# Cross attention with a routed FFN on one Trainium2 core: keys stacked by 12 transfers of four heads, q stacked through DRAM by 4, raw weights loaded later in the turn

## The reference

```python
x = x + xattn(layernorm(x), ctx)            # q and out: rows and weights quantized to 8-bit integers
    # q = w8a8(x, wq, bq); k = ctx @ wk.T + bk; v = ctx @ wv.T + bv     (16 heads of 32)
    # attn = softmax(q @ k.T / sqrt(32) + mask); out = w8a8(attn @ v, wo, bo)
x = x + moe(layernorm(x))
    # probs = softmax(h @ router_w.T); two best experts per token, their weights made to sum to 1
    # out += weight * (silu(h @ gate.T) * (h @ up.T)) @ down.T
```

## Time and profile before

| | |
|---|---|
| median of 3 runs | 1627.09 us (1625.84 to 1628.61) |
| the profiled execution | 1627.48 us, span of its instructions 1625.8 us |
| PE busy | 1506.3 us, 93% |
| DVE, ACT, POOL busy | 58%, 54%, 45% |
| attention loop (score matmuls) | 61.7 to 1118.4 us |
| experts | from 1168.7 us |
| moved by DMA | 281.53 MB, mean 173 GB/s |
| mean granted TensorE clock | 0.974 |

### The profile page before, as it was taken

One profiled execution on the slowest core, in us unless ns is written; L12 is line 12 of the kernel. 1 busy time (PEld: TensorE's weight loads), 2 busy tenths in 40 slices (PEclk: granted clock), 3 DMA queues, 4 the chain that ended last, 5 costly groups with the idle time before them and its releaser, 6 DMA issues. The chain is left out here.

```text
span 1625.8 us, 40635 instructions
## 1 busy us (share of the span) xinstructions
PE 1506.3 (93%) x11593; PEld 1312.3 (81%) x11594; DVE 944.7 (58%) x2675; ACT 878.9 (54%) x2128; POOL 731.8 (45%) x798
## 2 busy tenths in 40 slices
PE   2899999999999999999999999995299999999796
PEld 2788888888888888888888888874299999999695
DVE  6567777777777777777777777765222222222121
ACT  2466666666666666666666666664033333333232
POOL 4234444543445434543444434542445555555352
PEclk9999999999999999999999999997599999999898
DMA  6667777677667777677766776668147766575543
GB/s 201 171 171 204 202 207 184 176 220 199 188 178 193 208 201 185 175 219 197 192 180 188 213 201 187 175 178 264 33 77 181 184 162 142 141 171 121 134 78 46
DMA packets 219151, 281.53 MB, mean 173 GB/s; under 512 B 82080, under 2 KB 163872, under 8 KB 219104
## 3 DMA queue, kind: packets, MB, share of 16 engines
q1 hardware_dynamic: 200928, 247.78, 54.2%
q0 software_dynamic: 18176, 33.17, 11.4%
HBM read 118.12 MB, written 66.77 MB: 114 GB/s over the span
## 5 line engine op out<-in xcount | busy, mean ns | idle before, releaser
L500 ACT ACTIVATE probs<-probs,neg_max 112x375 f32<-112x375 f32 x512 | 311.8, 609 | 235.2 <-DVE neg_max L576 229.1
L576 DVE CUSTOM_DVE_ANT_0 probs<-score,neg_mask 112x375 f32<-112x375 f32 x512 | 279.3, 545 | 195.9 <-PE score L729 179.7
L493 ACT ACTIVATE probs_t<-turn 125x336 f32<-125x336 f32 x512 | 225.0, 440 | 99.8 <-PE turn L737 99.4
L737 PE MATMUL turn<-ident,probs 112*125 112x112 f32 x1536 | 265.7, 282 | 2.7 <-ACT probs L500 2.7
L737 PEld LDWEIGHTS turn<-ident,probs 112*125 112x125 f32 x1536 | 223.6, 189 | 37.6 <-issue 19.1
L729 PE MATMUL score<-k_stack,q_stack 96*112 96x376 f32 x512 | 208.5, 407 | 4.3 <-DMA q_stack<-q_lo 3.4
L764 PE MATMUL proj<-down_hi,gate_up_hi 128*128 128x376 f32 x512 | 176.2, 344 | 14.9 <-DVE gate_up_lo L601 13.7
L978 POOL DMA_INDIRECT out<-y_rows,entries x63 | 102.2, 1622 | 175.0 <-ACT y_rows L1004 136.9
L1016 DVE TENSOR_TENSOR a_lo<-a_ps,a_hi 128x384 fp32r<-128x384 f32 x63 | 35.1, 558 | 250.9 <-ACT a_hi L991 159.0
L764 PE MATMUL proj<-down_hi,gate_up_lo 128*128 128x376 f32 x512 | 172.1, 336 | 0.0
L764 PE MATMUL proj<-down_lo,gate_up_hi 128*128 128x376 f32 x512 | 172.0, 336 | 0.0
(11 more groups left out here) (195 smaller groups left out, 3552.7 us busy)
## 6 DMA issues: line engine op xcount, KB each, us to landing
k_stack<-gate_up_hi SPq DMA_DIRECT2D x512, 94.0 KB, 2.1
k_stack<-gate_up_lo SPq DMA_DIRECT2D x256, 94.0 KB, 2.1
ctx_stage<-ctx_t SPq DMA_DIRECT2D x32, 750.0 KB
q_stack<-q_hi SPq DMA_DIRECT2D x256, 56.0 KB, 2.0
w_raw<-gate_up_t SPq DMA_DIRECT2D x32, 352.0 KB, 3.1
gate_up_dram_hi<-w_hi SPq DMA_DIRECT2D x32, 352.0 KB
gate_up_dram_lo<-w_lo SPq DMA_DIRECT2D x32, 352.0 KB
gate_up_hi<-gate_up_dram_hi SPq DMA_DIRECT2D x16, 704.0 KB, 6.6
```

What stands on the lines that cost most here:

```text
L493: act.activation(probs_t[:, h % RING_T, :, :], turn[h % 2][0:LC, 0:LT * N].rearrange("p (l n) -> p l n", l=LT), ACT.Copy).then_inc(turned_ ...
L500: act.activation(probs[:, h % DS, :], probs[:, h % DS, :], ACT.Exp, bias=neg_max[:, par % 2, h:h + 1], scale=-1.0, accum_out=total[:, par ...
L576: dve.tensor_tensor_reduce(probs[:, h % DS, :], score[h % 2][0:N, 0:L], neg_mask[:, p, :], 1.0, BIG, ALU.add, ALU.min, neg_max[:, p, h:h + ...
L737: mm = pe.transpose(turn[h % 2][0:LC, l * N:(l + 1) * N], probs[:, h % DS, l * LC:(l + 1) * LC], W["ident"][0:N, 0:N])
```

## The change

Keys are stacked four heads at a time, by `stack_keys(i)` with three transfers for the heads 4i to 4i + 3. These four heads lie in the same 32 partitions, one in each key unit: the host orders the rows of wk, wq and their biases so that partition group i of all four units holds heads 4i to 4i + 3. Group 3 of element a is stacked at the top of turn a, groups 0, 1 and 2 of n in the middle, each when the four scores that read its place are done; all of them need all four key units. k_stacked becomes four semaphores of 3 transfers each, and ACT waits for all four before it writes k_hi at g = 0. q_hi and q_lo lie in one tile, which one transfer copies to DRAM between k(0) and k(1); three transfers of 32 partitions bring it back into q_st when the copy has landed. ACT waits for the copy (q_kept) before it writes q_hi again. The two loads of w_raw move from before neg_mask to behind x_res.

```diff
--- before.py
+++ after.py
@@ -210,7 +210,7 @@
                 mm.then_inc(row_made, 1)
 
 
-def attention(nc, W, R, x, ctx_t, mask, x1, h2, slots):
+def attention(nc, W, R, x, ctx_t, mask, x1, h2, slots, q_dram):
 
 
 
@@ -228,7 +228,7 @@
     UNITS = KT + LT
     GH = 4
     DS, RING_T = 4, 2 * GH
-    KDMAS, QDMAS = 12, 12
+    KDMAS, QDMAS = 3, 3
 
     with ExitStack() as ctx:
         sb = lambda name, shape, dt=F32: ctx.enter_context(nc.sbuf_tensor(name, shape, dt))
@@ -241,7 +241,8 @@
         stage, c_hi, c_lo, x_in = W["stage"], W["c_hi"], W["c_lo"], W["x_in"]
         k_hi, k_lo = [W[f"k_{part}"][:, 0:G4 * LP].rearrange("p (g l) -> p g l", g=G4) for part in ("hi", "lo")]
         k_st = sb("k_stack", [96, H, LP], F32R)
-        q_hi, q_lo = sb("q_hi", [128, G4, N], F32R), sb("q_lo", [128, G4, N], F32R)
+        q_parts = sb("q_parts", [128, 2, G4, N], F32R)
+        q_hi, q_lo = q_parts[:, 0, :, :], q_parts[:, 1, :, :]
         q_st = sb("q_stack", [96, 2, H, N], F32R)
         v = sb("v", [LC, 2, LT, C])
         neg_mask = sb("neg_mask", [N, 2, L])
@@ -290,10 +291,11 @@
 
         c_hi_made, c_lo_made = W["c_hi_made"], W["c_lo_made"]
         unit_made, unit_out = sem("unit_made"), sem("unit_out")
-        k_hi_made, k_stacked = sem("k_hi_made"), [sem("k_stacked0"), sem("k_stacked1")]
+        k_hi_made, k_stacked = sem("k_hi_made"), [sem(f"k_stacked{i}") for i in range(4)]
         ln1, rstd_made = sem("ln1"), sem("rstd_made")
         q_made, q_out = sem("q_made"), sem("q_out")
         q_biased, q_hi_made, q_stacked = sem("q_biased"), sem("q_hi_made"), sem("q_stacked")
+        q_kept = sem("q_kept")
         mask_negated = sem("mask_negated")
         scored, masked, softmaxed = sem("scored"), sem("masked"), sem("softmaxed")
         turned, turned_out, valued = sem("turned"), sem("turned_out"), sem("valued")
@@ -343,13 +345,12 @@
 
         @block.sync
         def _(sp):
-            def stack_keys(half):
-
-                for i in range(4):
-                    rows = slice(QUARTER * i, QUARTER * i + QUARTER)
-                    for r, src in ((0, k_hi), (1, k_lo), (2, k_hi)):
-                        sp.dma_start(k_st[QUARTER * r:QUARTER * r + QUARTER, 8 * half + i:8 * half + 8:4, :].bitcast(F32),
-                                     src[rows, 2 * half:2 * half + 2, :].bitcast(F32)).then_inc(k_stacked[half], 16)
+            def stack_keys(i):
+
+                rows = slice(QUARTER * i, QUARTER * i + QUARTER)
+                for r, src in ((0, k_hi), (1, k_lo), (2, k_hi)):
+                    sp.dma_start(k_st[QUARTER * r:QUARTER * r + QUARTER, G4 * i:G4 * i + G4, :].bitcast(F32),
+                                 src[rows, :, :].bitcast(F32)).then_inc(k_stacked[i], 16)
 
             def body(it, par, inside=False):
                 has_m2, has_m, has_a, has_n, has_nn, has_n3 = stages(it, inside)
@@ -359,11 +360,8 @@
                     if inside or it > 0:
                         waited(sp)
                         need(sp, scored, H * it)
-                    stack_keys(1)
+                    stack_keys(3)
                 if has_n:
-                    need(sp, w_lo_made, n)
-                    sp.dma_start(w_raw[:, 0:WG], W["gate_up_flat"][:, bass.ds(n * WG, WG)]).then_inc(w_in, 16)
-                    sp.dma_start(w_raw[:, WG:WG + WD], W["down_flat"][:, bass.ds(n * WD, WD)]).then_inc(w_in, 16)
                     need(sp, masked, H * (n - 1))
                     sp.dma_start(neg_mask[:, (par + 1) % 2, :], mask[n, :, :]).then_inc(mask_in, 16)
                 if has_m2:
@@ -375,18 +373,24 @@
                     need(sp, x1_steps, 2 * m)
                     sp.dma_start(x_res[:, :], x[m, :, :]).then_inc(x_res_ld, 16)
                 if has_n:
+                    need(sp, w_lo_made, n)
+                    sp.dma_start(w_raw[:, 0:WG], W["gate_up_flat"][:, bass.ds(n * WG, WG)]).then_inc(w_in, 16)
+                    sp.dma_start(w_raw[:, WG:WG + WD], W["down_flat"][:, bass.ds(n * WD, WD)]).then_inc(w_in, 16)
+                if has_n:
                     q = (par + 1) % 2
-                    need(sp, unit_out, UNITS * n + KT // 2)
-                    if has_a:
-                        waited(sp)
-                        need(sp, scored, H * it + H // 2)
-                    stack_keys(0)
-                    need(sp, q_out, 3 * n + 3)
-                    for i in range(4):
-                        rows = slice(QUARTER * i, QUARTER * i + QUARTER)
-                        for r, src in ((0, q_hi), (1, q_hi), (2, q_lo)):
-                            sp.dma_start(q_st[QUARTER * r:QUARTER * r + QUARTER, q, i:H:4, :].bitcast(F32),
-                                         src[rows, :, :].bitcast(F32)).then_inc(q_stacked, 16)
+                    need(sp, unit_out, UNITS * n + KT)
+                    for i in range(3):
+                        if has_a:
+                            waited(sp)
+                            need(sp, scored, H * it + G4 * (i + 1))
+                        stack_keys(i)
+                        if i == 0:
+                            need(sp, q_out, 3 * n + 3)
+                            sp.dma_start(q_dram[n, :, :, :], q_parts[:, :, :, :].bitcast(F32).rearrange("p a g n -> p a (g n)")).then_inc(q_kept, 16)
+                    need(sp, q_kept, 16 * (n + 1))
+                    for r, part in ((0, 0), (1, 0), (2, 1)):
+                        sp.dma_start(q_st[QUARTER * r:QUARTER * r + QUARTER, q, :, :].bitcast(F32).rearrange("p (i g) n -> p i (g n)", g=G4),
+                                     q_dram[n, :, part, :].rearrange("(i p) f -> p i f", p=QUARTER)).then_inc(q_stacked, 16)
                 if has_n3 and (inside or n3 > 0):
                     need(sp, c_lo_made, n3)
                     need(sp, c_hi_made, n3)
@@ -403,8 +407,8 @@
                     sp.wait_ge(unit_out, UNITS * B)
                     sp.wait_ge(w_stored, 64 * B)
                     load_expert(sp, R, 0)
-                    for half in range(2):
-                        sp.wait_ge(k_stacked[half], 16 * KDMAS * B)
+                    for i in range(4):
+                        sp.wait_ge(k_stacked[i], 16 * KDMAS * B)
                     load_expert(sp, R, 1)
 
             iterations(sp, body)
@@ -511,8 +515,9 @@
                     if h in (3, 5, 7, 9) and has_n:
                         g = h // 2 - 1
                         need(act, unit_made, UNITS * n + g + 1)
-                        if g % 2 == 0:
-                            need(act, k_stacked[g // 2], 16 * KDMAS * n)
+                        if g == 0:
+                            for i in range(4):
+                                need(act, k_stacked[i], 16 * KDMAS * n)
                         act.activation(k_hi[:, g, :], proj[(par + 1 + g) % 2][:, 0:LP], ACT.Identity,
                                        bias=W["bk_col"][:, g:g + 1]).then_inc(k_hi_made, 1)
                     if has_a:
@@ -528,7 +533,7 @@
                                        ACT.Copy).then_inc(r_out, 1)
                     if h == 9 and has_n:
                         need(act, q_made, 3 * n + 3)
-                        need(act, q_stacked, 16 * QDMAS * n)
+                        need(act, q_kept, 16 * n)
                         act.activation(q_hi[:, :, :], misc[:, 0:G4 * N].rearrange("p (g n) -> p g n", g=G4),
                                        ACT.Identity).then_inc(q_hi_made, 1)
                     if h == 10 and has_nn and (inside or nn > 0):
@@ -721,8 +726,8 @@
         def _(pe):
             def scores(b, par, h):
                 k = b * H + h
-                if h % 8 == 0:
-                    need(pe, k_stacked[h // 8], 16 * KDMAS * (b + 1))
+                if h % G4 == 0:
+                    need(pe, k_stacked[h // G4], 16 * KDMAS * (b + 1))
                 if h == 0:
                     need(pe, q_stacked, 16 * QDMAS * (b + 1))
                 need(pe, masked, k - 1)
@@ -1139,7 +1144,7 @@
                                                                         "slots_cleared", "pads_cleared")})
             prepare_weights(nc, W, x, ctx_t, wq, wk_t, wv_t, wo, bq, bk, bv, bo, router_t, slots, h2, out[T:T + PAD_ROWS, :])
             attention(nc, W, R, x, ctx_t, mask, out[0:T, :].rearrange("(b n) c -> b n c", n=N),
-                      h2[0:T, :].rearrange("(b n) c -> b n c", n=N), slots)
+                      h2[0:T, :].rearrange("(b n) c -> b n c", n=N), slots, dram("q_parts_dram", (B, 128, 2, C // 128 * N)))
         experts(nc, W, R, h2, slots, out)
 
 
@@ -1155,9 +1160,10 @@
 
     turn = lambda a, *axes: np.ascontiguousarray(np.transpose(np.asarray(a), axes))
     whole = lambda a: np.ascontiguousarray(np.asarray(a))
+    by_chunk = lambda a: np.asarray(a).reshape(4, 4, -1).swapaxes(0, 1).reshape(np.asarray(a).shape)
     arrays = {
         "x": whole(x), "ctx_t": turn(ctx_2048, 0, 2, 1), "mask": whole(mask_BxSxS2_ff0),
```

(2 more changed lines are left out.)

## The result

The changed kernel takes 1799.63 us (median of 4 runs, 1793.39 to 1801.81) against 1626.46 us for the kernel before, run beside it: a ratio of 1.106, 95% interval 1.103 to 1.109. The prediction was 1691 us with a range of 1642 to 1748. Slower was right, for the reason given; the size was not, and the result is outside the range. The profiled execution took 1799.6 us with a span of 1797.9, the one before 1627.5 and 1625.8, so 172.1 us are to be explained.

A forecast was written before the change was run, and what follows sets the result against it. PE's work was taken to bound the attention loop. The profiled 1627.5 us, plus 64.8 for the gaps (30 x 2.0 + 4.8) as k(3) lands late, less 1.6 at the end, gave 1691 us; range 1642 to 1748.

The forecast's parts named there:

- (e): ACT's k_hi write at h = 3 now waits for all four stackings; DVE's low part and PE wait behind it.
- (f): SP's queue, moved in order, lands k(3) 21.7 us after the fourth result; low part 2.0 us late each turn.
- 0.2 late, inside the 2.0: q loads land 0.2 us after the score matmul's time, within the 2.0 us stall per turn and not on top.
- The first gap and the end: First gap between fourth and next first result grows 4.8 us; expert loads reached earlier at the end give -1.6 us.
- The clock, a rival at 0.32: PE's clock falls behind its pauses in the loop, losing 1.7 us in each of 31 turns, 53 us: 1744; chance 0.32.
- (a): SP's issuing: 24 key and 12 q transfers become 12 and 4; worth nothing inside the loop.
- the first rival: No stall: above 272 GB/s into 32 partitions k(3) is in time and the change no slower, 1627; chance 0.12.
- (b): Two raw weight loads issued behind the mask, the x1_s and h2_s stores and the x_res load: nothing.
- (c): Host order of the weights' rows, q_lo and q_hi in one tile: same instructions and shapes, nothing.
- (d): ACT waits before q_hi for the copy to DRAM, which comes before the old stacking: nothing.
- faster: Third rival: line 601 at h = 3 comes earlier, PE's 0.4 us per turn goes, 12 us in all: 1614; chance 0.06.

The follow-up runs named there:

- with q ahead: Changed kernel with its three q loads issued ahead of k(2), k(3) left at the top of the next turn: 1864.59 us, 1.142 of before.
- the kernel with the order mended: Changed kernel with k(3) issued at the end of the turn before and the q loads ahead of k(2): 1623.66 us, 0.998 of before.
- the swap on DVE: Kernel before with DVE's two operations at h = 3 exchanged, the keys' low part ahead of h2_s: 1610.78 us, 0.990 of before.

## Why the prediction was right or wrong

**(e), the wait that moves: right.** ACT waits at h = 3 for k_stack in 25 turns (57.1 us), DVE and PE behind it (57.2 us, some 70 predicted), and the chain hangs on the fourth result of the turn before. The wait alone on the kernel before (1863.5) and k(3) a turn earlier (1708) show it from both sides.

**(f), when k(3) lands: the failed step.** 21.7 us were predicted from the fourth result to k(3)'s landing, and a gap of 22.9. Measured are 23.7 us to the last byte, some 24.3 to the landing (ACT's write begins at 928.44, 24.3 after 904.12), and a gap of 25.5. Two terms were too small.

First the way to k(3)'s first byte: 18.6 us in the sum (21.7 less 2.5 for k(3)'s data and 0.6 for its landing), 19.5 in the trace. By the times of the single pieces (medians over 27 turns) this is lost at the head of the chain: k(0)'s 0.58 MB last from 1.4 to 4.9 us behind the fourth result, 3.6 us where 2.5 were taken, and the copy ends at 6.4 instead of 5.1. Why k(0) is slow stays open. From there on the stretches are as long as they were taken: k(1) and k(2) end at 11.1 (10.0 in the sum), q's loads at 14.1 (13.0). So the 230 GB/s, from 154 GB/s divided by a share of 0.64 and its like, were too much for k(0) (205) and not for k(1) and k(2) (238). The Trainium skill, SBUF — State Buffer, section on the DMA port swizzle, has 218 GB/s as the asymptote into 32 partitions; k(0) stays under it, k(1) and k(2), six such transfers one behind the other into three groups of 32 partitions, do not. For such a train the measured 238 decides.

Second and larger, k(3) itself: 2.5 us at 230 GB/s, measured 4.2 (its first piece begins 19.5 us behind the fourth result, its last ends at 23.7). "SP's transfers are moved in order" is what failed. In the stretch from 923.6 to 927.8 the engines move 257 GB/s x 4.2 us = 1.08 MB, of which k(3) has 0.58. The mask and the store of x1_s, issued behind it at 921.72 and 923.45, move 0.35 MB beside it, which at 257 GB/s is 1.4 of the 1.7 us; the other 0.15 MB are the last of the weight stores ahead of it. With the raw weights behind it as well k(3) ends 0.9 us later. The Trainium skill, DMA: Bandwidth & Descriptors, section on queues, rings and completion order, says that on each DMA engine descriptors are consumed in ring order but a later one may finish its write first, and that completion is not in order for an issuing engine; the trace agrees as far as it goes (mask pieces move from 925.5 on, k(3)'s last one begins at 927.2), and shows that this has a price for the earlier transfer.

**"0.2 late, inside the 2.0": half right.** q was 2.1 us late in the turn (score matmul 15.3 us behind the fourth result, not 13.2): its loads ended 14.1 us behind it instead of 13.0, and from the last byte to the matmul it is 1.2 us, of which the prediction had 0.4. But inside the chain it was: with q ahead the gaps stay, and only the place of the pause changes.

**The first gap and the end.** +4.8 was predicted for the first gap, 7.1 measured; -1.6 for the end, -4.6 measured behind the last score matmul. The last element was forgotten, with its wait for q and its clock (+4.9). Together they make little.

**The clock, a rival at 0.32: real, but of another size.** It was priced at 1.7 us in each of 31 turns, 53 us, and cost 24 us in 7 turns through the stretches, as most falls of the clock began before k(3)'s pause. The 108.9 us between the sum (1690.7) and the profiled execution (1799.6) are 82.8 us of gaps (147.6 less 64.8), 24.2 of the stretches that the clock made longer, and 1.9 behind the last result (0.3 instead of -1.6).

**(a) "worth nothing": wrong for the chain.** On the kernel before only q's part of it was run alone (0.997); the keys' part was not. Where the chain starts at the fourth result, transfers of 94 KiB cost 69 us more. So coalescing, which the Trainium skill, DMA: Bandwidth & Descriptors, rules for kernel authors, advises, did help here; but the first rival ("above 272 GB/s") fell with the 205 and 238 measured. **(b) "Nothing": the same.** Moving the raw loads gives 0.999 alone on the kernel before; with the new wait in place it is worth 65 us. Both terms were priced by the slack of the kernel before, which step (e) of the same prediction had used up. **(c), (d): right**, as the kernel with the order mended, at 0.998, holds them all.

**The sign.** For faster there was 0.07. Its mechanism exists, though the change doesn't use it: the swap on DVE shows that PE's 0.4 us per turn are to be had (1.0%).

## What to carry to other kernels

When a change makes a wait stand on the last transfer of a chain, price every other part of the change again in that chain: transfers issued just behind it slow it, and the time to issue those ahead counts. A rate seen with idle engines, divided by their share, is no measurement: 240 GB/s was worked out so, and 205 and 238 came. And before removing one of two pauses, ask where the clock's fall behind the remaining one will lie: order the queue by who waits first (here q, k(2), k(3), then loads and stores), which removes both.

## What had not been expected of the hardware

Pauses of PE of about 2 us in an otherwise full loop already bring its clock to half (behind 1.8 to 2.0 us in about every second turn, with k(3) a turn earlier), and a longer one costs more. Two pauses of about 2 us per turn lengthened the stretches by 24 us in the whole loop; one of 4.65 us, with 0.50 granted for 9.2 us behind the one shown, by 82. The place changed with the length, and no run separates the two fully; with keys in transfers of two heads, one pause of some 4.6 us per turn at q cost nothing in the stretches but took the loop's clock to 0.92. The Trainium skill, TensorE: Matmul & The Clock Gate, section on HAM oscillation, describes a wait in every tile that sends each next tile off cold; the trace agrees (0.50 behind the pause shown), and suggests that the price depends on what hangs on the matmuls behind the pause.

Transfers of one issuing queue, k(3) and the ones behind it, share the DMA engines though the second of those is issued 2.7 us behind the last of k(3)'s three (920.75 and 923.45): 4.2 us for k(3), two thirds more than its bytes alone at 230 GB/s. And into 32 partitions transfers of 188 KiB moved 205 to 238 GB/s at full share, those of 94 KiB 149 GB/s at 0.64, by the 0.63 us that SP takes to issue one.
